# Down products of a mixture-of-experts chunk issued two chunks behind the up products instead of one

## The reference

```python
x = x + tanh(g_xattn[0]) * _L0_xattn_ref(_layernorm(x), ctx, ...)   # 8 experts, top 2, relu; routed by ctx
x = x + tanh(g_ffn[0])   * _L0_ffn_ref(_layernorm(x), ...)          # 4 experts, top 2, gated by silu
x = x + tanh(g_xattn[1]) * _L1_xattn_ref(_layernorm(x), ctx, ctx, mask, ...)  # attention, 16 heads of 8
x = x + tanh(g_ffn[1])   * _L1_ffn_ref(_layernorm(x), ...)          # gated MLP, 352 wide, inputs quantised to fp4
```

```python
h = silu(einsum('td,edf->etf', xf, w1)) * einsum('td,edf->etf', xf, w3)
expert_out = einsum('etf,efd->etd', h, w2)
out = einsum('te,etd->td', gates, expert_out)
```

## Time and profile before

| what | value |
|---|---|
| median of 3 runs | 1255.24 us |
| the profiled execution, its own time | 1258.71 us |
| its span from first to last instruction | 1256.9 us |
| granted TensorE clock over the span | 0.87 |
| PE busy | 982.3 us (78% of the span) |
| DVE busy | 753.0 us (60%) |
| ACT busy | 626.6 us (50%) |
| POOL busy | 582.6 us (46%) |

### The profile page before, as it was taken

The page is one execution under the profiler, slowest core; times in us unless marked ns, Lnnn a source line. Parts: engine busy times, 40 slices in busy tenths (PEclk is TensorE's granted clock), DMA queues, the critical chain, the costliest instruction groups (busy, mean ns, idle before and its releaser), DMA issues.

```text
span 1256.9 us, 17423 instructions
## 1 busy us (share of the span) xinstructions
PE 982.3 (78%) x5204; PEld 702.5 (56%) x5204; DVE 753.0 (60%) x1764; ACT 626.6 (50%) x1875; POOL 582.6 (46%) x637
## 2 busy tenths in 40 slices
PE   6440899990686997888889798888988888887772
PEld 6220688880454665565566566556656656654551
DVE  3525476662374685787578577657857867654232
ACT  2531466650242765655555565655555655644440
POOL 2477433332546247446444653634555354531213
PEclk9965799995798999989988998998899999967565
DMA  9799587646101001021102102100210200200000
GB/s 281 236 357 343 178 285 252 239 179 87 22 1 27 8 5 35 7 30 24 22 6 33 34 8 36 26 14 10 30 37 5 36 10 7 36 5 11 7 4 5
DMA packets 126513, 93.66 MB, mean 75 GB/s; under 512 B 77546, under 2 KB 105684, under 8 KB 121684
## 3 DMA queue, kind: packets, MB, share of 16 engines
q1 hardware_dynamic: 121268, 82.05, 24.4%
q0 software_dynamic: 4096, 8.40, 2.5%
q10 hardware_dynamic: 1056, 2.10, 0.6%
HBM read 59.46 MB, written 33.06 MB: 74 GB/s over the span
## 4 chain that ended last, share of the span: by engine, by line
PE 45%; POOL 22%; DVE 12%; issue 10%; ACT 9%; DMA 2%; SPq 0%; POOLq 0%; DVEq 0%; ACTq 0%
ACT pr L764 6%; PE U L1119 5%; POOL xs_dram L511 5%; POOL yg L563 5%; PE M L1316 5%; PE U L1123 4%; PE U L1120 4%; PE M L1322 4%; POOL h_lo L572 4%; PE M L1349 3%; DVE xin L962 3%; PE Y L1123 2%; PE M L1313 2%; PE M L1361 2%; PE Y L1119 2%
## 5 line engine op out<-in xcount | busy, mean ns | idle before, releaser
L572 POOL TENSOR_TENSOR h_lo<-h,h_hi 128x512 fp32r<-128x512 f32 x128 | 164.9, 1289 | 240.4 <-ACT h_hi L735 240.0
L764 ACT ACTIVATE pr<-M,nmax 128x128 f32<-128x128 f32 x512 | 180.7, 370 | 51.2 <-DVE nmax L1058 50.9
L729 ACT ACTIVATE h<-U 128x512 f32<-128x512 f32 x128 | 76.4, 597 | 147.1 <-PE U L1123 146.8
L1058 DVE TENSOR_REDUCE nmax<-M 128x4 f32<-128x512 f32 x128 | 87.4, 683 | 87.3 <-PE M L1316 86.7
L1119 PE MATMUL U<-xn_hi,w_hi 128*128 128x512 f32 x256 | 126.0, 492 | 8.2 <-DVE h L1007 6.4
L1003 DVE SCALAR_TENSOR_TENSOR h<-h,U 128x512 f32<-128x512 f32 x128 | 87.6, 684 | 74.6 <-ACT h L729 74.4
L1322 PE MATMUL M<-ident,pr 128*128 128x128 f32 x512 | 87.4, 298 | 54.5 <-ACT pr L764 54.4
L1123 PE MATMUL U<-xn_lo,w_hi 128*128 128x512 f32 x256 | 108.9, 426 | 0.0
L1120 PE MATMUL U<-xn_hi,w_lo 128*128 128x512 f32 x256 | 108.6, 424 | 0.0
L1322 PEld LDWEIGHTS M<-ident,pr 128*128 128x128 f32 x512 | 62.7, 151 | 81.8 <-issue 62.7
L764 ACT ACTIVATION_READ_ACCUMULATOR pr<-M,nmax 128x1 f32 x512 | 107.4, 210 | 0.0
(11 more groups left out here) (307 smaller groups left out, 2328.8 us busy)
## 6 DMA issues: line engine op xcount, KB each, us to landing
wt<-w_dram SPq DMA_DIRECT2D x23, 1024.0 KB, 4.8
w_dram<-wt SPq DMA_DIRECT2D x8, 1024.0 KB, 8.6
xs_dram<-xr SPq DMA_DIRECT2D x1, 5888.0 KB, 20.7
ys_dram<-acc SPq DMA_DIRECT2D x12, 256.0 KB, 2.3
key_stack<-k_dram SPq DMA_DIRECT2D x48, 64.0 KB
wt<-k_dram SPq DMA_DIRECT2D x48, 64.0 KB
ys_dram<-part SPq DMA_DIRECT2D x11, 256.0 KB, 2.3
pr<-in_L_xattn_W SPq DMA_DIRECT2D x8, 256.0 KB, 6.6
```

The source lines that it names most:

```text
L572: nc.gpsimd.tensor_tensor(h_lo[i % 4][:, :], h32[i % 3][:, :], h_hi[i % 4][:, :].bitcast(fp32), ALU.subtract).then_inc(lo_done, 1)
L764: done = nc.scalar.activation(pr[i % 2][:, c], bank[:, c], ACT.Exp, bias=nmax[i % 4][:, r:r + 1], accum_out=rsum[b % 2][:, HB * r + j:HB * ...
L1058: nc.vector.tensor_reduce(nmax[i % 4][:, :], m_bank(("s", i))[0][:, :].rearrange("p (h k) -> p h k", h=HB), AX.X, ALU.max, negate=True).th ...
```

## The change

A function `later` adds to the sort key of some steps: 6 units, one chunk, for `down` of chunks 0 to 13 of a group and for `combine` and `acc` of the first three experts; 3 units for `down` of chunk 14; nothing for chunk 15 and the last expert's sum. PLACED is empty. Nothing else differs: the same instructions with the same waits, in another order on PE, DVE and POOL; the orders of ACT and SP are as they were.

```diff
+PLACED = {}
+LAG1 = 6.0
...
+def later(what, i):
+
+    if what == "down" and i % N1 < N1 - 2 or what in ("combine", "acc") and i % E1 < E1 - 1:
+        return LAG1
+    return LAG1 / 2 if what == "down" and i % N1 == N1 - 2 else 0
...
+    timed = [(PLACED.get((what, i), t + later(what, i)), what, i) for t, what, i in timed]
     return [(what, i) for _, what, i in sorted(timed, key=lambda e: e[0])]
```

## The result

Over 20 runs each the changed kernel took a median of 1251.18 us (1247.88 to 1256.2) and the kernel before 1260.62 (1250.05 to 1267.64). The ratio is **0.9938, with a 95% interval of 0.9917 to 0.9959**: faster by 0.6%, about 7.8 us. The forecast was 12.7 us of 1255.2, or 1.0%. The kernel before was slower over its 20 runs than in the first three of them, shown ahead of the prediction, so only ratios are compared from here on. The sign was right and the waits of `down` went, as forecast; the gain came out 5 us smaller. As far as the traces show, that is because the forecast counted PE's matmuls at the same duration before and after.

The account below looks back on a forecast made before the run. PE was taken as the fullest engine, its waits as what reordering can win. The terms -6.7 - 2.6 + 1.2 + 1.8 - 2.6 - 3.8 = -12.7 us took 1255.2 to 1242.5 us; range 1234 to 1253.

Parts of the forecast that it names:

- First group and turn, -2.6 and -3.8: First group: one ring turn won at chunk 2's 8.42 us wait, -2.6 us; turn to the second group: shorter waits, -3.8.
- Chunk 1: nothing: `down`'s 1.49 us wait for `lo` goes, but `nxT` still needs nxn from DVE, so no gain.
- Chunk 2, five turns: -6.7: `down`'s 1.33 us wait for `lo` behind the gathers ends in turns from group 2 to 6: 5 x 1.33 us.
- Chunk 12: -2.6: `down`'s 0.43 us wait goes in six groups, with a `pt` behind that did not wait: 6 x 0.43 us.
- The other moved sums: nothing: First and third experts' `combine` fall into DVE's wait or `pt`'s slack; POOL's additions change places with `lo`: no cost.
- `mix`: +1.8: `combine` now stands between `swiglu` and `mix`, so `mix` ends 0.26 us later in seven groups: 7 x 0.26 us.
- Group end: +1.2: An extra `down` between `pt` and `s` delays `up`, partly hidden at POOL: 0.2 us each, six times.
- handed on: Rival, 13%: in groups 2 to 7 PE meets the next late thing each time; -6.7 and -2.6 fall away: 1251.8 us.
- The clock rival: Rival, 9%: gathered idle gaps cost two more slow-clock chunks in each of seven groups, +30.8 - 12.7: 1273 us.

Follow-up runs that it names:

- the six other kernels with this order of PE: The change with sums placed differently (once also late `down`s), PE's order in the turns kept: ratios to the kernel before 0.9813, 0.9814, 0.9957, 0.9805, 0.9896, 0.9723.
- the last three kernels: The change with third sum and second `acc` behind: 0.9723; also one `down` behind `qs`: 0.9638; also a `down` between `nxT` and `q`: 0.9648.

## Where the prediction was right, and the step that failed

The waits of `down` went as forecast: PE idles 11.0 us less, where the sum has 12.7. The step that failed is that the sum counted removed idle time at its full value and the change of the granted clock at nothing. Term by term:

- *First group and turn, -2.6 and -3.8.* -6.3 forecast for the stretch, -6.6 measured, by other parts than I gave, so the closeness is luck. The 8.42 us became 6.66, not 5.8, and the next `up` that `mix` holds back waits 3.50 us instead of 1.64:

```profile
335.38 0.80 PE L1133 MATMUL Y<-h_lo,w_hi 128*128 128x512 f32 x1 [6.66 <-POOL h_lo L582]
...
357.10 0.50 PE L1129 MATMUL U<-xn_hi,w_hi 128*128 128x512 f32 x1 [3.50 <-DVE h L1013]
```

- *Chunk 1: nothing.* Right: `nxT` waits for nxn instead.
- *Chunk 2, five turns: -6.7.* **This step failed.** The wait went, and a turn at full clock is shorter by about what I said; but the sum priced PE's matmuls at the same duration before and after. In the profiled pair 7.6 of the 9.4 us of idle time came back as slower matmuls, and 1.8 us were gained. That execution is at the unfavourable end: the six other kernels with this order of PE gained 2.1 to 6.4 us in their turns, with PE idle for 7.6 to 10.8 us less and busy for 1.9 to 8.7 longer. None reached 6.7; the mean of the seven is 4.3.
- *Chunk 12: -2.6.* The sign was right by accident. I followed the 0.43 us to the next `pt` and not to the `f_xt` behind it, which now waits 1.80 us; the clock of that stretch rose from 0.77 to 1.00 and paid for more than that.
- *The other moved sums: nothing.* Right against their old place (0.9957 with the third sum unmoved). I treated them as neutral, and they were the best handle in the table: 1.2% for one POOL instruction per group.
- *`mix`: +1.8.* The idle time behind it grew from 2.75 to 2.92, by 0.17 where I had 0.26, and `mix` itself fell from 5.96 to 5.49 us behind `combine`: the picture of pieces that queue behind POOL's work held. What I had not asked is what that work costs. `acc` stretched `mix` by a microsecond in the change and stood beside it before too, and the low clock behind the wait was paid in both kernels.
- *Group end: +1.2.* The stretch from `f_xt` to `nxT` took 125.9 us in five groups against 124.6, 0.26 each where I had 0.2. That is chance: one pass at 0.94 took 26.5 us, and the four others 24.8 or 24.9 as before, so at full clock the term is nothing.
- *The rivals.* Waits were handed on in part: `pt` +4.5 and `f_xt` +10.0 us. The clock rival had the right sign, at a sixth of its price (some 5 us, where it had 30.8). I gave it 9% as a case by itself, where it was a term that belonged into the sum. The mean granted clock was 0.864 in the change's 20 runs, and 0.867 in the 46 runs of the kernel before beside the experiments (its 20 runs beside the change carry no clock). From PE's 982 us that is an estimated 982 x 0.0036 / 0.867 = 4.1 us, which is about what the forecast missed.

That the clock changes PE's time is shown where a stretch without idle time changes its length (behind `mix`) and at the turn. What decides whether a given turn runs low isn't shown: turns with the same waits ran at 0.83 and at 1.00 in one execution. Whether the 5 us of the last two stretches recur in other runs of the change stays open as well, since only one execution of it has a trace; the mean clock of its runs fits.

## What to carry to other kernels

Price PE's waits with the clock behind them: look at the granted clock and PE's busy time of the stretch that follows a wait, in several passes and in several traces, before counting a wait at its own length; the same order of PE was busy for 122.0 to 128.8 us in five turns. When a step is moved, ask also what its companions on other engines run beside; moving one POOL addition of 1.3 us, for which no matmul waits soon, gained more than the whole change. And follow a removed wait past the next late input to the one after it.

## What was not expected of the hardware

- One and the same kernel's time follows the granted clock from run to run: single runs of the kernel before took 1266.88 us at a mean clock of 0.858 and 1252.22 at 0.876, a spread nearly twice the change's gain.
- Waits of two sizes around one place differ by more than their lengths: in the change some 2.9 us were followed by 0.73 to 0.85, with the second `acc` behind 1.92 by 0.85 or 1.00, and in the last three kernels 1.9 also by 0.73 or 0.74. The Trainium skill (TensorE: Matmul & The Clock Gate, section "Why this matters for your kernels") says to leave no idle gaps between bursts of matmuls, because the clock falls back to half. The rows behind `mix` agree in most passes; behind `f_xt`'s 1.80 us in the change the next stretch ran at 1.00 in four groups of five, so a gap alone doesn't settle it.
